# Expert tiles of two sizes in a decoder layer: 31 tiles of 256 rows and nine of 128, half tiles with the rows stationary, routing counts made earlier

## The chip, the core and the metric

One core of one Trainium2 chip runs the whole program. The metric is the device time of one execution in microseconds (us). The core has TensorE (PE), VectorE (DVE), ScalarE (ACT), GpSimd (POOL) and the sync engine (SP), which here only issues DMAs.

## What is computed

A decoder layer over 32 sequences of 128 tokens, 256 channels (4096 tokens): self attention, cross attention, then a block with self attention and a mixture of experts, each followed by a layer norm. The part that the change touches is the mixture:

```python
logits = h2 @ router_w                                   # 8 experts
topw, topi = jax.lax.top_k(jax.nn.softmax(logits), 2)
topw = jax.nn.softmax(topw)
shared = silu(h2 @ sh_gate) * (h2 @ sh_up) @ sh_down     # d_ff 512
gate, up = h2 @ e_gate[e], h2 @ e_up[e]
eout[e] = (silu(gate) * up) @ e_down[e]
X + shared + sum over the token's two experts of topw * eout[e]
```

Matrix products are kept near float32 by splitting both factors into a rounded part (`_hi`) and a rest (`_lo`) and adding three products: hi x hi, hi x lo, lo x hi.

## The kernel before

`phase_a` does the attention stages, and stores each token's normalized row (`h2`) and the residual sum. `phase_b` is the mixture. Its work is cut into 55 **units** of 256 rows (`UT`): 13 units of the shared expert (`BEFORE`), 39 **tiles** of the routed experts (`TILES` = 2 x 4096 / 256 + 8 - 1), 3 more shared units. A tile holds rows of one expert only; since the counts of an expert are known only at run time, 39 tiles are enough for any routing, and an expert's last tile can be partly empty.

While the first shared units run, DVE chooses the two experts of each token (`choose_first`, `choose_second`), weighs them (`weigh`), and takes each token's rank in its expert from two matmuls that PE issues after the first unit (`ranked`). `count_tiles` and `find_slots` turn the ranks into slot numbers (`slot_index`), `place` makes the table of each tile's expert. POOL then scatters the 8192 rows by indirect DMA into `slots_scratch` (64 DMAs, L1554), each batch of four behind a count of gate-and-up halves. SP loads a tile's rows (`load_slots`) and its expert's three weight matrices, 1.5 MB (`load_expert`), three sets of raw weights deep.

All engines walk the units in the same order, each in its own program:

- PE, unit n: `gate_up(n, 0)` (gate and up for the first 256 of the 512 hidden channels; weights stationary, 256 rows moving), `turn(n + 1)` (four transposes of the next rows), `gate_up(n, 1)`, `down_unit(n - 1)` (two row blocks of 128, `act` stationary, weights moving).
- ACT: `silu_half(n, 0)`, `token_hi(n + 1)`, `product_hi(n, 0)`, `split(n, 2)`, `split(n + 1, 0)`, `split(n + 1, 1)` (the rounded parts of the weights), `silu_half(n, 1)`, `product_hi(n, 1)`.
- DVE: `product(n, 0)` (silu times up, L1450), `read_down(n - 2)` (for a tile: scaled by the token's weight, L1473), `token_lo(n + 1)`, `split_lo(n, 2)`, `split_lo(n + 1, 0)`, `split_lo(n + 1, 1)` (L1434), `product(n, 1)`.
- POOL, in tiles: `routed_lo(n, 0)` (`act_lo`, L1569), `add_tile(i - 2)` (two indirect DMAs that add a tile's rows into `total_scratch`, L1580, each tile's behind the landing of all earlier ones), `routed_lo(n, 1)`.

After the tiles the sums are loaded back into `acc`, normalized pair by pair (DVE moments, POOL root, ACT scaling) and stored.

## Time and profile before

| | |
|---|---|
| median of 3 runs | 1155.63 us (1154.27 to 1155.94) |
| the profiled execution | 1154.84 us, its span 1153.0 us |
| PE busy | 1076.8 us, 93% of the span |
| DVE, ACT, POOL busy | 805.8 (70%), 620.1 (54%), 551.0 (48%) us |
| attention stages, then the mixture | up to 617.8 us, from there on |
| the 13 first shared units, the 39 tiles | 617.8 to 742.3 us, 742.3 to 1100.4 us |

The profile is of one execution; its rows give for each engine what ran when, and what an idle time before an instruction ended with (`<-`). A pair such as 128x256 is partitions by elements. "x12" are twelve instructions merged into one row. In the rows, tiles that live in freed places carry the name of the place: `kept_weights` can be the silu result or a tile's rows, `kept_late` the scaled rows of a tile, `h_rows`, `raw_gate` and `w_raw` raw expert weights, `turned` the transposed rows.

### The profile page before, as it was taken

What the parts mean: (1) busy time and instruction counts of PE and PEld (TensorE: products, weight loads), DVE (VectorE), ACT (ScalarE), POOL (GpSimd) and SP (SyncE); (2) the same over time, 40 slices, a digit from 0 to 9 for tenths busy, and PEclk for the clock granted to TensorE, in tenths of its full rate; (3) what the DMA queues carried; (4) which work ended last, traced back from release to release, by engine and by line L of the source; (5) the groups of instructions that cost most, each with busy time, mean ns of one, the idle gap of its engine ahead of it and who ended that gap; (6) DMA issues with size and microseconds to landing.
All of it is one profiled execution on the core that took longest, in us unless ns stands there. A gap on an engine that the chain in (4) does not pass through costs nothing. (4 is left out here: it accounts for less than half of the span.)

```text
span 1153.0 us, 32693 instructions
## 1 busy us (share of the span) xinstructions
PE 1076.8 (93%) x13012; PEld 1011.7 (88%) x13012; DVE 805.8 (70%) x1367; ACT 620.1 (54%) x1266; POOL 551.0 (48%) x542
## 2 busy tenths in 40 slices
PE   3789999999999999999966999999999999999992
PEld 2678889989898989898865999999999999999992
DVE  1668778777778777788645644577777777777746
ACT  1244555555555555566544333466666666666635
POOL 4243334344343344434201477346666666666754
PEclk8999999999999999999986999999999999999996
DMA  7585455454654444541215422368878887878548
GB/s 211 101 192 106 94 95 107 114 115 91 131 111 91 120 108 74 103 71 35 93 38 167 165 102 97 125 202 230 239 232 236 231 226 219 224 233 230 139 76 244
DMA packets 294679, 167.73 MB, mean 145 GB/s; under 512 B 220688, under 2 KB 266000, under 8 KB 293648
## 3 DMA queue, kind: packets, MB, share of 16 engines
q1 hardware_dynamic: 278064, 141.05, 45.5%
q0 software_dynamic: 14880, 22.09, 9.4%
q10 hardware_dynamic: 1584, 2.49, 0.6%
q8 instruction: 104, 1.70, 0.6%
q14 instruction: 47, 0.39, 0.1%
HBM read 121.74 MB, written 54.15 MB: 153 GB/s over the span
## 5 line engine op out<-in xcount | busy, mean ns | idle before, releaser
L1580 POOL DMA_INDIRECT total_scratch<-kept_late,slot_meta x78 | 135.4, 1736 | 110.6 <-DMA total_scratch<-kept_late,slot_meta 58.5
L1450 DVE TENSOR_TENSOR prod<-kept_weights,up 128x512 f32<-128x512 f32 x110 | 75.2, 683 | 144.2 <-ACT kept_weights L1290 144.2
L1569 POOL TENSOR_TENSOR act_lo<-prod,act_hi 128x512 fp32r<-128x512 f32 x78 | 120.3, 1686 | 36.5 <-ACT act_hi L1297 36.5
L1297 ACT ACTIVATE act_hi<-prod 128x512 fp32r<-128x512 f32 x110 | 69.5, 632 | 111.1 <-DVE prod L1450 109.7
L1290 ACT ACTIVATE kept_weights<-gate 128x512 f32<-128x512 f32 x110 | 64.8, 589 | 110.6 <-PE up L1221 110.6
L678 ACT ACTIVATE p3t<-psum 128x512 f32<-128x512 f32 x128 | 68.8, 596 | 89.2 <-PE psum L527 89.2
L929 POOL TENSOR_TENSOR ctx_lo<-ctx_t,ctx_hi 128x512 fp32r<-128x512 f32 x16 | 20.6, 1288 | 139.8 <-ACT ctx_hi L588 139.8
L849 DVE TENSOR_REDUCE max<-psum 128x16 f32<-128x2048 f32 x32 | 73.3, 2292 | 18.2 <-PE psum L513 18.2
L368 PE MATMUL psum<-kept_room,x_hi 128*128 128x512 f32 (+1 forms) x256 | 62.4, 367 | 18.3 <-POOL x_lo L925 18.3
L1274 ACT ACTIVATE we_hi<-w_raw 128x1024 fp32r<-128x1024 f32 x78 | 77.7, 1044 | 0.0
L1221 PE MATMUL gate<-tok_hi,we_hi 128*128 128x256 f32 x312 | 67.7, 298 | 1.2 <-DVE we_lo L1434 0.7
L368 PEld LDWEIGHTS psum<-kept_room,x_hi 128*128 128x128 f32 x256 | 42.3, 197 | 25.7 <-issue 21.4
L872 DVE RECIPROCAL rden<-psum 128x256 f32<-128x256 f32 x32 | 56.2, 1757 | 10.1 <-PE psum L540 10.1
L1554 POOL DMA_INDIRECT slots_scratch<-h_rows,slot_index x56 | 55.0, 982 | 16.7 <-issue 12.5
L1221 PE MATMUL up<-tok_lo,we_hi 128*128 128x256 f32 x312 | 62.8, 283 | 0.0
L1221 PE MATMUL up<-tok_hi,we_hi 128*128 128x256 f32 x312 | 62.6, 282 | 0.0
L1221 PE MATMUL gate<-tok_lo,we_hi 128*128 128x256 f32 x312 | 62.5, 282 | 0.0
L1434 DVE TENSOR_TENSOR we_lo_place<-w_raw,we_hi 128x1024 fp32r<-128x1024 f32 x39 | 53.7, 1403 | 1.2 <-ACT we_hi L1274 0.3
L1434 DVE TENSOR_TENSOR we_lo<-w_raw,we_hi 128x1024 fp32r<-128x1024 f32 x39 | 53.4, 1396 | 1.2 <-ACT we_hi L1274 0.3
L925 POOL TENSOR_TENSOR x_lo<-x_t,x_hi 128x512 fp32r<-128x512 f32 x16 | 20.5, 1278 | 66.3 <-ACT x_hi L584 66.2
L1221 PEld LDWEIGHTS gate<-tok_hi,we_hi 128*128 128x128 f32 x312 | 47.6, 190 | 4.8 <-issue 3.8
L1237 PE MATMUL down<-we_hi,act_hi 128*128 128x256 f32 x312 | 50.2, 283 | 0.0
(277 smaller groups left out, 3404.7 us busy)
## 6 DMA issues: line engine op xcount, KB each, us to landing
w_raw<-in_w_gate SPq DMA_DIRECT2D x26, 512.0 KB, 3.6
w_raw<-in_w_up SPq DMA_DIRECT2D x26, 512.0 KB, 4.5
w_raw<-in_w_down SPq DMA_DIRECT2D x26, 512.0 KB, 6.2
slots_scratch<-in_empty SPq DMA_DIRECT2D x39, 258.0 KB, 3.8
kept_weights<-slots_scratch SPq DMA_DIRECT2D x39, 258.0 KB, 6.0
raw_gate<-in_w_gate SPq DMA_DIRECT2D x13, 512.0 KB, 3.6
h_rows<-in_w_up SPq DMA_DIRECT2D x13, 512.0 KB, 4.5
h_rows<-in_w_down SPq DMA_DIRECT2D x13, 512.0 KB, 6.2
```

Of the source, the lines that this page charges most:

```text
L368: mm = pe.matmul(dst, x(dk), y(dk), start=(n == 1), stop=(n == 3 * DK))
L678: act.activation(p3t[:, a, 4 * j:4 * j + 4, :], bank[f"s3t_{a}"][:, 512 * j:512 * (j + 1)].rearrange("p (h n) -> p h n", h=4), ACT.Exp)\
L849: half_step(dve.tensor_reduce(max3[:, a, :], bank[f"s3_{a}"].rearrange("p (h n) -> p h n", h=H), AX.X, ALU.max, negate=True))
L872: half_step(dve.reciprocal(rden3[:, a, :], bank[f"pv3_{a}"][:, DK * S:2 * DK * S]))
L1221: mm = pe.matmul(bank[:, fi * UT:(fi + 1) * UT], wp[:, kind, dk * DFF + f * P:dk * DFF + (f + 1) * P], hp[:, n % 2, dk, :], start=(m == 1) ...
L1274: act.activation(w_hi[:, kind, :], raw_of(use)[kind], ACT.Copy).then_inc(w_hi_done, 1)
L1290: act.activation(silu[:, h, :], gate[h][:, :], ACT.Silu).then_inc(silu_done, 1)
L1297: act.activation(act_hi[:, n % 2, h * FH:(h + 1) * FH, :], prod[:, h, :].rearrange("p (f n) -> p f n", f=FH), ACT.Copy).then_inc(act_hi_do ...
L1434: dve.tensor_tensor(w_lo[:, kind, :], raw_of(use)[kind], w_hi[:, kind, :].bitcast(F32), ALU.subtract).then_inc(w_lo_done, 1)
L1450: dve.tensor_tensor(prod[:, h, :], silu[:, h, :], up[h][:, :], ALU.mult).then_inc(prod_done, 1)
L1569: pool.tensor_tensor(act_lo[:, n % 2, h * FH:(h + 1) * FH, :], prod[:, h, :].rearrange("p (f n) -> p f n", f=FH), act_hi[:, n % 2, h * FH: ...
L1580: pool.indirect_dma_start(out=scratch["total"], out_offset=bass.IndirectOffsetOnAxis(ap=slot_meta[:, i % METAS, j, 0:1].bitcast(I32), axis=0),
```

## The change

The routed experts get `FULL` = 31 tiles of 256 rows and `HALF` = 9 tiles of 128 rows, 40 tiles and 56 units. An expert's rest of up to 128 rows goes to a half tile, a larger rest to a full tile while there are full ones left, else to two half ones. `ORDER` runs four full tiles, then nine times three full ones and a half one.

In a half tile, `gate_up` keeps the 128 rows stationary and moves 256 columns of weights, so its result has rows on the partitions; the products are computed in that form, `turn_products` (new, PE) transposes them, four transposes into the bank `turned`, and `half_hi` (ACT) and `half_lo` (DVE, from PSUM) take the place of `product_hi`, `product_lo` and of POOL's `routed_lo`. `turn_products(n)` stands at the end of unit n on PE, behind `down_unit(n - 1)`. A half tile has one row block in `turn`, `down_unit`, `read_down` and `add_tile`.

The counting is longer (two kinds of tiles), and `count_tiles` moves from unit 1's first half to unit 0's second half, behind `weigh`. The list of steps also fills 36 pieces of empty slots in place of 39.

```diff
-TILES = 2 * B * S // UT + E - 1
+FULL = 2 * B * S // UT - 1
+HALF = E + 1
+TILES = FULL + HALF
-ROWS = TILES * UT
+ROWS = FULL * UT + HALF * P
+EMPTY = -(-ROWS // UT)
...
+        ORDER = [*range(FULL - 3 * HALF), *(x for h in range(HALF) for x in (*range(FULL - 3 * (HALF - h), FULL - 3 * (HALF - h) + 3), FULL + h))]
...
+        def product_read(k):
+            n = k // 2
+            return (act_turned, halves_upto(n)) if is_half(n) else low_products(k)
...
+                        if is_half(n - 2):
+                            pe.wait_ge(half_lo_done, halves_upto(n - 2))
-                        for j in range(2):
+                        for j in range(parts_of(n)):
...
+                        if is_half(n):
+                            for m, (wp, hp, dk) in enumerate(terms):
+                                at = dk * DFF + h * FH * P
+                                mm = pe.matmul(bank[:, 0:FH * P], hp[:, n % 2, dk, 0:P], wp[:, kind, at:at + FH * P],
+                                               start=(m == 0), stop=(m == 3 * DK - 1))
+                            continue
...
+                def turn_products(n):
+                    pe.wait_ge(prod_done, 2 * n + 2)
+                    for f in range(FT):
+                        mm = pe.transpose(turned[n % 2][:, f * P:(f + 1) * P], prod[:, f // FH, f % FH * P:(f % FH + 1) * P], ident[:, :])
+                    mm.then_inc(act_turned, 1)
...
+                    if is_half(n):
+                        turn_products(n)
...
+                def half_hi(n):
+                    act.wait_ge(act_turned, halves_upto(n))
+                    act.wait_ge(down_ready, n - 1)
+                    act.activation(act_hi[:, n % 2, :, 0:P], turned[n % 2][:, :].rearrange("p (f n) -> p f n", f=FT), ACT.Copy)\
+                       .then_inc(act_hi_done, 2)
...
-                    product_hi(n, 0)
+                    if not is_half(n):
+                        product_hi(n, 0)
...
-                    product_hi(n, 1)
+                    if is_half(n):
+                        half_hi(n)
+                    else:
+                        product_hi(n, 1)
...
+                    step_of_route(dve.scalar_tensor_tensor(out=f["rest"], in0=f["full"], scalar=-float(UT), in1=count,
+                                                           op0=ALU.mult, op1=ALU.add))
+                    step_of_route(dve.tensor_scalar(f["large"], f["rest"], float(P), None, ALU.is_gt))
...
+                    step_of_route(dve.tensor_tensor(further, slot[:, :, :], by_token("full_rows"), ALU.is_ge))
+                    step_of_route(dve.tensor_tensor(further, further, by_token("half_base"), ALU.mult))
+                    step_of_route(dve.tensor_tensor(slot[:, :, :], slot[:, :, :], by_token("full_base"), ALU.add))
+                    step_of_route(dve.tensor_tensor(slot[:, :, :], slot[:, :, :], further, ALU.add))
...
-                ROUTING = {(0, 0): (choose_second,), (0, 1): (weigh,), (1, 0): (count_tiles, find_slots), (1, 1): (place,)}
+                ROUTING = {(0, 0): (choose_second,), (0, 1): (weigh, count_tiles), (1, 0): (find_slots,), (1, 1): (place,)}
...
+                def half_lo(n):
+                    dve.wait_ge(act_hi_done, 2 * n + 2)
+                    dve.tensor_tensor(act_lo[:, n % 2, :, 0:P], turned[n % 2][:, :].rearrange("p (f n) -> p f n", f=FT),
+                                      act_hi[:, n % 2, :, 0:P].bitcast(F32), ALU.subtract).then_inc(half_lo_done, 1)
...
                     product(n, 1)
                     if i is None:
                         product_lo(n, 1)
+                    elif is_half(n):
+                        half_lo(n)
...
-                    routed_lo(n, 0)
+                    if not is_half(n):
+                        routed_lo(n, 0)
                     if i >= 2:
                         add_tile(i - 2)
-                    routed_lo(n, 1)
+                    if not is_half(n):
+                        routed_lo(n, 1)
```

## Rows read from the trace of the kernel before

**Rows 1.** Busy time by stretch: PE, PEld, DVE, ACT, POOL; clock, DMA share, GB/s.
```profile
617.00:644.00 27.00, 23.20 (x155) 22.82 (x156) 20.97 (x48) 11.16 (x17) 1.63 (x2) 0.82 0.41 132
...
860.00:940.00 80.00, 79.98 (x663) 78.85 (x663) 59.64 (x80) 50.80 (x79) 53.09 (x36) 1.00 0.82 234
```

**Rows 2.** Chain that ended last, first tile: start us, us, what.
```profile
742.50 1.44 PE gate L1221 x12
...
745.82 1.43 PE gate L1221 x12
...
748.69 2.88 PE down L1237 x24
751.57 1.42 PE gate L1221 x12
```

**Rows 3.** PE in order of time: start us, us, instruction, count, [idle before, releaser].
```profile
736.09 0.66 PE L1201 MATMUL turned<-ident,kept_weights 128*128 128x128 f32 x4 [1.02 <-DMA slot_meta<-slots_scratch]
...
742.34 0.40 PE L1221 MATMUL gate<-tok_hi,we_hi 128*128 128x256 f32 x2
...
1100.43 0.40 PE L1221 MATMUL gate<-tok_hi,ws_hi 128*128 128x256 f32 x2
```

**Rows 4.** DVE in order of time, the first tile and one in the middle.
```profile
746.05 0.69 DVE L1450 TENSOR_TENSOR prod<-kept_weights,up 128x512 f32<-128x512 f32 x1 [2.58 <-ACT kept_weights L1290]
...
748.39 1.48 DVE L1434 TENSOR_TENSOR we_lo<-w_raw,we_hi 128x1024 fp32r<-128x1024 f32 x1 [0.26 <-ACT we_hi L1274]
749.79 2.35 DVE L1434 TENSOR_TENSOR we_lo_place<-w_raw,we_hi 128x1024 fp32r<-128x1024 f32 x2
752.06 0.68 DVE L1450 TENSOR_TENSOR prod<-kept_weights,up 128x512 f32<-128x512 f32 x1
...
882.34 0.69 DVE L1450 TENSOR_TENSOR prod<-kept_weights,up 128x512 f32<-128x512 f32 x1 [2.16 <-ACT kept_weights L1290]
...
884.68 1.86 DVE L1434 TENSOR_TENSOR we_lo_place<-w_raw,we_hi 128x1024 fp32r<-128x1024 f32 x1
...
888.73 0.68 DVE L1450 TENSOR_TENSOR prod<-kept_weights,up 128x512 f32<-128x512 f32 x1
```

**Rows 5.** ACT in order of time, around the start of a tile.
```profile
880.21 0.63 ACT L1297 ACTIVATE act_hi<-prod 128x512 fp32r<-128x512 f32 x1 [2.21 <-DVE prod L1450]
881.71 0.60 ACT L1290 ACTIVATE kept_weights<-gate 128x512 f32<-128x512 f32 x1 [0.87 <-PE up L1221]
```

**Rows 6.** POOL in order of time, the same tile and the next.
```profile
879.06 1.95 POOL L1580 DMA_INDIRECT total_scratch<-kept_late,slot_meta  x1 [2.84 <-DMA total_scratch<-kept_late,slot_meta]
881.31 1.55 POOL L1580 DMA_INDIRECT total_scratch<-kept_late,slot_meta  x1 [0.30 <-issue]
882.32 3.12 POOL L1569 TENSOR_TENSOR act_lo<-prod,act_hi 128x512 fp32r<-128x512 f32 x2
888.12 2.13 POOL L1580 DMA_INDIRECT total_scratch<-kept_late,slot_meta  x1 [2.68 <-issue]
```

**Rows 7.** DVE and POOL in order of time, the routing.
```profile
638.03 0.68 DVE L1389 TENSOR_TENSOR_SCAN w_raw<-w_raw,down 128x256 f32<-128x256 f32 x1
...
640.30 0.17 DVE L1400 TENSOR_TENSOR_SCAN tiles_upto<-w_raw,n_tiles 128x8 f32<-128x8 f32 x1
640.51 0.17 DVE L1404 TENSOR_TENSOR first_row<-tiles_upto,n_tiles 128x8 f32<-128x8 f32 x1
...
644.02 0.19 POOL L1549 COPY kept_rows<-row_w 128x4 f32<-128x4 f32 x1 [25.17 <-DVE slot_index L1412]
```

**Rows 8.** POOL, then DVE, in order of time behind the tiles.
```profile
1113.39 1.55 POOL L1580 DMA_INDIRECT total_scratch<-kept_late,slot_meta  x1 [0.30 <-issue]
1117.37 3.65 POOL L1598 DMA_DIRECT2D acc<-total_scratch  x4 [2.43 <-DMA total_scratch<-kept_late,slot_meta]
...
1131.12 0.69 DVE L1467 TENSOR_TENSOR acc<-down,acc 128x512 f32<-128x512 f32 x1 [0.85 <-PE down L1237]
...
1139.30 0.75 DVE L1482 BATCH_NORM_STATS2 stats_b<-acc 128x6 f32<-128x256 f32 x2 [1.02 <-DMA acc<-total_scratch]
```

More of the change, by code:

```diff
@@ L1036, in phase_b @@
         past = late[:, E * SHARED:E * SHARED + TILES * E].rearrange("p (i e) -> p i e", e=E)
+        few = {n: sb(n, [P, E]) for n in ("full", "full_upto", "rest", "large", "large_upto", "grown", "half", "half_upto", "over",
+                                          "full_base", "half_base", "full_rows")}
         expert_iota = c["expert"].rearrange("p (b e) -> p b e", e=E)
@@ L1231, in down_unit @@
                         pe.wait_ge(down_read, n - 1)
-                    for j in range(2):
+                    for j in range(parts_of(n)):
                         m = 0
@@ new lines, in count_tiles @@
+                    step_of_route(dve.scalar_tensor_tensor(out=f["half"], in0=f["rest"], scalar=0.0, in1=f["large"],
+                                                           op0=ALU.is_gt, op1=ALU.add))
+                    step_of_route(dve.scalar_tensor_tensor(out=f["half"], in0=f["grown"], scalar=-2.0, in1=f["half"],
+                                                           op0=ALU.mult, op1=ALU.add))
+                    step_of_route(dve.tensor_tensor(f["full"], f["full"], f["grown"], ALU.add))
```

115 lines of the change are left out of this document (73 added, 42 removed).

## The prediction

> **What bounds the kernel now.** I read three views in order. First the busy time by stretch [rows 1]: in the middle of the expert tiles PE is busy for the whole stretch at the full clock, DVE three quarters of it, and the DMA engines 0.82. So the stage is PE's, if nothing holds PE back unseen. Second, the chain of work and PE's own order of time [rows 2, 3]. A unit of 256 rows is a first gate-and-up half with the turning of the next rows (742.50 to 745.82, 3.32), a second one (2.87) and the products down of the unit before (2.88): 9.07 us. The 39 tiles take 1100.43 - 742.34 = 358.1 us, 9.18 each. Third, DVE's order of time [rows 4], because a PE that is always busy may have another engine running exactly as fast. The product `prod` of the first half starts 3.71 after the unit (742.34 to 746.05), that of the second half 6.01 later (to 752.06), or 6.39 later (882.34 to 888.73). Between them DVE scales the rows of the tile two before, makes `tok_lo` and splits three weight matrices, 1.14 each when alone (2.35 for two). The next unit may start when the second of these three is done: 3.71 + 6.01 - 1.14 + 0.1 for the signal = 8.7, or 9.05 in the longer form. This loop through PE, ACT and DVE is only 0.0 to 0.4 us shorter than PE's own work. That is what the reader is to see: a stage with 100% of PE busy and a second bound right beneath it, which does not shrink with the rows of a tile, since it is made of weight splits.
>
> Why two forms: the subtraction of POOL (L1569) and the first split of DVE overlap. In the short form that split takes 1.48, in the long form 1.86, where POOL ran two subtractions in one piece until 885.4 [rows 4, 6]. The Trainium skill, page "SBUF — State Buffer", section "Who interferes with whom", says that a DVE instruction with two SBUF inputs blocks, and is blocked by, a GpSimd instruction that reads SBUF; by that rule the trace agrees, and `half_lo`, which reads PSUM and SBUF, would not collide.
>
> **The tiles.** The 39 units become 31 full ones and nine half ones: four full, then nine times three full and one half. I call the half one H, the full ones behind it F1, F2 and F3.
>
> PE alone: a half tile has 12 + 12 matmuls of gate and up instead of 48, 12 down instead of 24, and 4 + 2 transposes instead of 4. By [rows 2] that is 1.44 + 1.44 + 1.44 + 0.44 + 0.22 = 4.98 against 9.07. If PE alone counted, the stage would be 31 x 9.05 + 9 x 4.98 = 325.4, some 33 us less. I don't take it, for this reason.
>
> H: its PE sequence is gate-and-up 1.44, turning 0.44, gate-and-up 1.44, then the *full* products down of F3 (2.88), then the new `turn_products`, which waits for both products. In front of the second product stand, in DVE's program, all three splits. The working: `prod` of F3's second half starts 3.71 + 6.01 to 6.39 - 0.28 (its `tok_lo` is for a half tile) = 9.44 to 9.82 after F3's start, that is 0.6 to 1.0 into H. Then come this product (0.68), `act_hi` (0.63, partly overlapped) and the silu of H, 0.35 as half of the 0.60 [rows 5]: 1.6 in sum. From the first to the second product of H: 6.01 - 0.27 for the half product - 0.27 as POOL has no subtraction of H, 5.5; at worst 6.1. Product 0.43, four transposes 0.44. Sum: 8.6 to 9.6 us, against PE's own 6.6. I take 8.8, near the lower end, because only the one subtraction for F3 is left in H and it starts at H + 3 at the latest by [rows 6] if an add holds it less than now. PE's queue behind the waiting transpose is the first gate of F1; who waits for it is everybody.
>
> F1 has the short products down (1.44 less), so PE needs 7.6; but its splits are whole: 8.7 by the loop. F2: PE 9.05 with an occasional delay, 9.1; its scaling of H's rows is 0.4 shorter, which nobody feels. F3: 9.05 less two transposes 0.22 = 8.83, the loop 8.8; I take 8.85. Group: 8.8 + 8.7 + 9.1 + 8.85 = 35.45, bounds 34.9 and 36.3. The stage: 4 x 9.05 = 36.2, plus 9 x 35.45 = 319.05, plus 0.35 (the first F1 has no H before it), less 1.0 (the last H has no splits of a next tile in front of its product) = **354.6, against 358.1: -3.5 us**. So nearly all of the 33 us is spent on 40 tiles' splits instead of 39, each at the pace of the loop.
>
> What hides the rest: the forty weight loads. A group has four loads in 35.4 us, now four in 36.7, and 3.5 instead of 4 tiles of slots and adds; the share of 0.82 [rows 1] stays where it is, and loads are issued two and a half units ahead. SP's `load_slots` behind H's early `load_expert` may wait up to 3 us for an add; the rows are needed over 10 us later. The adds of POOL: each must land before the next, 881.31 to 888.12, 6.8 us, and with two issues a tile makes 879.06 to 888.12, 9.06 [rows 6]; this chain is as long as a unit too. H's tile has one issue, 2.25 less, so per group it is 4 x 9.06 - 2.25 = 34.0, within 35.45. If that cover goes, see the second rival.
>
> **The start.** `count_tiles` began at 638.03 and is now done behind `weigh`, 632.3. It has ten small steps more, and `find_slots` nine small ones in place of two, of 0.21 each (640.30 to 640.51), and three more over 256 columns, 0.45 each [rows 7]. From 632.3: the old part 2.3 and 2.1 of new steps, 636.7; then the product, `tok_lo` and `act_lo` that stood in front before (2.1), 638.8; then 1.9 + 1.8 + 2.5 = 6.2, 645.0. The slot numbers, for which POOL waits until 644.02, were there at 643.9: **+1.1 us** (bounds 0 and +2.5, as a step on an [128, 8] tile with a column operand is in no row). All of it counts: POOL's 64 scatters follow without a pause, and PE waits for the first rows (1.02, [rows 3]).
>
> **The tail.** The last tile is a half one; its products down stand in the first shared unit behind the tiles: PE is 1.44 earlier, and the `acc` of DVE at 1131.12 with it. The last adds: one issue less at their end, and about 4 us earlier against PE's unit, so the wait of 1.02 for the sums [rows 8] goes; DVE and ACT are next. **-2.4 us** (bounds 0 and -2.5). The 36 instead of 39 fills of empty slots lie in the first stage beside PE's work: nothing.
>
> **Sum.** -3.5 + 1.1 - 2.4 = -4.8. The profiled execution is 1154.84 (span 1153.0, 1.84 around it), 0.8 under the median 1155.63: span 1148.2, that execution 1150.0, median **1150.8**.
>
> **Rivals.**
> 1. The long form everywhere, and H at 9.45 (slower). POOL's subtraction for F3 starts only when its add is issued, 881.31 + 1 = unit + 3.7, and then meets the first split of H as it does now [rows 4, 6]. Group 36.3: +7.7, 1158.5. For it: the long form holds through most of the tiles. Against: the chain of adds gets 1.4 us of air per group. It decides from a group of 35.98 on, where the sum is zero.
> 2. One add per load burst. If an add lands when the burst of weights ends, as two of 6.8 suggest beside lone ones at the tail (1113.39 to 1117.1, [rows 8]), a unit can't be under 9.2: 40 x 9.2 - 1.4 = 366.6, 12 more, 1162.8.
> 3. PE's clock. The granted clock is 0.82 in a stretch where PE idles 3.8 of 27 us [rows 1]. H leaves PE idle for some 2 us in two pieces. If each H put the next twelve matmuls to the lower level, 1.2 GHz, they would take 2.88 instead of 1.44 [rows 2], 9 x 1.44 = 13 more at most: 1163. Against: the 1.02 us of wait at 736.09 was followed by gates of 1.44 at 742.50, the full clock [rows 2, 3]. The Trainium skill, page "TensorE: Matmul & The Clock Gate", Part 1, says that the slow clock is the default and that activity releases it; no run here shows yet which of the two an H is.
> 4. PE's own work sets the pace after all: 325.4, 1121. It needs DVE to be some 3.3 us earlier in H and 1.1 in F1, and no row shows such room.
> 5. The short form throughout, H 8.5: group 35.0, 1146.7.
>
> **How the numbers follow.** Forecast with its own bounds (1146 to 1154) 0.46; rival 1, partly reached in many mixtures (1154 to 1160), 0.27; rival 2, 0.08; rival 3, 0.03; rival 4, 0.04; rival 5, 0.12. A measurement of this kernel tells about 0.2% (2.3 us) from no change, 1153.3 to 1157.9. Faster: nine tenths of the forecast, rivals 4 and 5, 0.58; same: the forecast's last tenth and over half of rival 1, 0.20; slower: the rest of rival 1, rivals 2 and 3, 0.22. The range takes rival 1 and the better end of the others: 1144 to 1162; its own for the forecast is 1146 to 1154.
>
> **What would show it.** In the changed kernel PE must be idle before `turned<-prod` for about a microsecond in each H, released by DVE's `prod`; an H must take 8.6 to 9.1, F1 8.7; DVE's first split 1.2 to 1.5 in H and F1. The scatter must begin at about 646; the chain must have no 1.02 wait for `acc`. Wrong would be: H near 6.6, F1 near 7.6 (rival 4), a granted clock under 1 in the tiles (rival 3), or a wait of PE for `act_lo` in front of the products down (rival 2).

## The result, and the profile after

The change makes the kernel slower: 1162.26 us median over 15 runs beside 1155.94 for the kernel before, ratio 1.0056 with the interval [1.0041, 1.0071]; the forecast was 1150.8, its range 1144 to 1162. One run of each kernel took far longer (2603.03 and 2117.05 us) and is in the medians but not in the ratio; the others lie from 1157.85 to 1166.54 and from 1154.18 to 1157.59. The profiled execution took 1158.89, its span 1157.0. It is one of the shorter ones, so the profile shows less of the loss than the median.

| span of the profile, us | before | after | difference | forecast |
|---|---|---|---|---|
| up to the first tile | 742.34 | 743.62 | +1.3 | +1.1 |
| the tiles | 358.1 | 362.9 | +4.8 | -3.5 |
| behind the tiles | 52.6 | 50.5 | -2.1 | -2.4 |

The execution takes 1.9 us more than its span, as before (1.84). Start and tail came nearly as forecast; the error is in the tiles. Read from the starts of the units (the first `gate` of each in PE's order of time), the 40 tiles take, in us (H in bold; ahead of the first group stand four full ones of 9.06, 9.01, 9.04, 8.98):

| F1 | F2 | F3 | H |
|---|---|---|---|
| 9.03 | 9.24 | 8.87 | **10.71** |
| 8.90 | 9.23 | 8.88 | **10.48** |
| 8.88 | 9.07 | 8.82 | **8.75** |
| 8.88 | 9.08 | 8.81 | **8.75** |
| 8.89 | 9.08 | 8.81 | **8.78** |
| 8.95 | 9.07 | 8.82 | **8.75** |
| 8.88 | 9.08 | 8.81 | **9.74** |
| 8.88 | 9.08 | 8.81 | **10.48** |
| 10.24 | 9.24 | 8.90 | **7.14** |

So the undisturbed group is 8.88 + 9.08 + 8.81 + 8.75 = 35.5, against 35.45 forecast. Four H, the late ones from here on, are longer by 1.96, 1.73, 0.99 and 1.73, and one F1 by 1.36: 7.8 us, which is nearly the whole distance between 354.6 and 362.9. (The last H has no next tile to split weights for, and is short as forecast.)

**The H that went as forecast, and the one that did not.** PE in order of time in the changed kernel (start us, us, instruction, count, [idle before, releaser]), first the late H that starts at 806.85:

```profile
808.72 0.60 PE L1235 MATMUL turned<-ident,kept_weights 128*128 128x128 f32 x4
...
812.77 0.71 PE L1281 MATMUL down<-we_hi,act_hi 128*128 128x256 f32 x4 [2.03 <-issue]
...
813.83 1.06 PE L1281 MATMUL down<-we_hi,act_lo 128*128 128x256 f32 x4
...
817.21 0.60 PE L1267 MATMUL turned<-ident,prod 128*128 128x128 f32 x4
```

and the same places in the H that starts at 881.82:

```profile
886.38 0.71 PE L1281 MATMUL down<-we_hi,act_hi 128*128 128x256 f32 x4 [0.67 <-issue]
890.16 0.66 PE L1267 MATMUL turned<-ident,prod 128*128 128x128 f32 x4 [0.67 <-DVE prod L1549]
```

The second one has the wait that I looked for, 0.67 us for DVE's `prod` ahead of the new transposes, and the length that I gave it. But even here PE also waits 0.67 before the products down; in the late one that is 2.03. What it waits for stands in POOL's order of time, the same two tiles:

```profile
807.95 1.56 POOL L1685 DMA_INDIRECT total_scratch<-kept_late,slot_meta  x1 [3.46 <-DMA slot_meta<-slots_scratch]
809.81 1.56 POOL L1685 DMA_INDIRECT total_scratch<-kept_late,slot_meta  x1 [0.30 <-issue]
810.81 1.86 POOL L1675 TENSOR_TENSOR act_lo<-prod,act_hi 128x512 fp32r<-128x512 f32 x1
...
880.85 2.25 POOL L1685 DMA_INDIRECT total_scratch<-kept_late,slot_meta  x1 [1.39 <-DMA slot_meta<-slots_scratch]
883.41 1.56 POOL L1685 DMA_INDIRECT total_scratch<-kept_late,slot_meta  x1 [0.30 <-issue]
884.42 1.86 POOL L1675 TENSOR_TENSOR act_lo<-prod,act_hi 128x512 fp32r<-128x512 f32 x1
```

The second `act_lo` of F3 stands behind F1's add (the add of the tile two before), and that behind the landing of the adds before it. It starts 2.6 us into the normal H and 3.96 into the late one, and ends at 812.67 there; PE starts down at 812.77. In a full unit the products down stand 6.2 behind its start and there is room for this; in H they stand behind only 3.9 us of work. (`issue` as releaser hides it: PE's program waits there for `act_lo`.)

**What the late `act_lo` costs at the full clock.** Not this wait. In the H of 9.74, which starts at 1024.01 and waits 1.80 at down, PE is done with down and then still waits for DVE's second product:

```profile
1033.34 0.66 PE L1267 MATMUL turned<-ident,prod 128*128 128x128 f32 x4 [0.55 <-DVE prod L1549]
```

POOL's `act_lo` and DVE's first split in this H, then the same split in the normal one:

```profile
1027.73 1.86 POOL L1675 TENSOR_TENSOR act_lo<-prod,act_hi 128x512 fp32r<-128x512 f32 x1
1028.47 2.21 DVE L1532 TENSOR_TENSOR we_lo_place<-w_raw,we_hi 128x1024 fp32r<-128x1024 f32 x1
...
886.28 1.22 DVE L1532 TENSOR_TENSOR we_lo_place<-w_raw,we_hi 128x1024 fp32r<-128x1024 f32 x1
```

The split is begun beside the subtraction and ends 1.09 behind its end (1029.59), as if it had run after it. It takes 1.0 us more than in the normal H (2.21 beside 1.22), the product behind it starts 1.0 later (8.87 behind the start of H, 7.86 in the normal one), and H is 1.0 longer. The four late H have this split at 2.44, 2.21, 2.21 and 2.21, no other H has it over 1.22. This is the meeting of rival 1, in four groups of nine.

**The clock.** Busy time by stretch: PE, PEld, DVE, ACT, POOL; clock, DMA share, GB/s; the products down of the H of 10.71 in two pieces, those of the normal one, and those of the H of 9.74:

```profile
812.80:815.20 2.40, 2.40 (x15) 2.40 (x16) 2.40 (x3) 0.51 (x2) 0.00 (x0) 0.69 0.67 106
815.20:817.20 2.00, 2.00 (x11) 2.00 (x11) 1.16 (x2) 0.00 (x0) 1.55 (x1) 0.52 0.69 227
886.40:890.10 3.70, 3.09 (x24) 2.88 (x24) 3.70 (x4) 1.87 (x3) 0.00 (x0) 1.00 1.14 275
1029.70:1033.30 3.60, 3.09 (x24) 2.89 (x24) 3.59 (x4) 0.76 (x2) 0.00 (x0) 1.00 0.94 189
```

In the H of 10.71 the granted clock falls to about the half (1.2 GHz) about a microsecond after PE is back from its wait, and the 24 matmuls take 4.44 us, where they take 2.84 in a full unit (804.01 to 806.85). Here the wait at down does count: the slow products end behind `prod`, and `turned<-prod` has no wait (817.21). The clock fell in three of the four late H (waits of 2.03, 1.79 and 1.79), and not in the fourth (1.80): 10.48 beside 9.74.

**The F1 of 10.24.** POOL adds the tile F2 of the last group but one; the second issue of that add falls into F1 of the last group, and the `act_lo` behind it onto a split of DVE:

```profile
1069.47 1.56 POOL L1685 DMA_INDIRECT total_scratch<-kept_late,slot_meta  x1 [3.37 <-DMA total_scratch<-kept_late,slot_meta]
1077.16 1.55 POOL L1685 DMA_INDIRECT total_scratch<-kept_late,slot_meta  x1 [6.13 <-issue]
1078.17 1.84 POOL L1675 TENSOR_TENSOR act_lo<-prod,act_hi 128x512 fp32r<-128x512 f32 x1
1078.34 2.76 DVE L1532 TENSOR_TENSOR we_lo_place<-w_raw,we_hi 128x1024 fp32r<-128x1024 f32 x1
```

and PE's first row of the next tile, F2:

```profile
1081.24 0.47 PE L1259 MATMUL gate<-tok_hi,we_hi 128*128 128x256 f32 x2 [2.39 <-DVE we_lo_place L1532]
```

Between the two issues of one tile's add there is 0.30 us of idle time everywhere else (809.81, 883.41). Here it is 6.13, and the profile names no reason. I call it the held DMA; it was in none of my steps, and the later experiments are about it.

**What stayed.** The rest answers to rows of the kernel before. The stretches of [rows 1]:

```profile
617.00:644.00 27.00, 22.39 (x156) 21.87 (x157) 24.54 (x64) 11.84 (x18) 1.79 (x2) 0.83 0.43 138
860.00:940.00 80.00, 73.99 (x607) 72.27 (x606) 57.85 (x82) 50.71 (x81) 47.27 (x30) 1.00 0.77 223
```

PE's wait for the first rows, as in [rows 3]:

```profile
737.37 0.66 PE L1235 MATMUL turned<-ident,kept_weights 128*128 128x128 f32 x4 [1.27 <-DMA slot_meta<-slots_scratch]
```

DVE's last step of the slot numbers and POOL's first one behind it, as in [rows 7] (two rows, one of each engine's order of time):

```profile
644.76 0.18 DVE L1508 CAST slot_index<-row_slot 128x32 int32<-128x32 f32 x1
...
645.06 0.19 POOL L1655 COPY kept_rows<-row_w 128x4 f32<-128x4 f32 x1 [25.46 <-DVE slot_index L1508]
```

POOL's last add and first load of the sums, as in [rows 8]:

```profile
1117.80 1.55 POOL L1685 DMA_INDIRECT total_scratch<-kept_late,slot_meta  x1 [3.07 <-DMA total_scratch<-kept_late,slot_meta]
1122.40 3.67 POOL L1705 DMA_DIRECT2D acc<-total_scratch  x4 [3.05 <-DMA total_scratch<-kept_late,slot_meta]
```

and DVE's first sum of the last units, and its wait for the sums:

```profile
1135.84 0.69 DVE L1571 TENSOR_TENSOR acc<-down,acc 128x512 f32<-128x512 f32 x1 [0.85 <-PE down L1281]
1143.53 0.75 DVE L1586 BATCH_NORM_STATS2 stats_b<-acc 128x6 f32<-128x256 f32 x2 [0.53 <-DMA acc<-total_scratch]
```

In 860 to 940, which holds no late H, PE is busy 74.0 of 80 us where it was 80.0: the work that the half tiles save is there as idle time, and the stage does not run faster for it.

### The profile page after: what moved, and what is told of

Its sections match the earlier page's. It is cut to its first block and busy times, and to the rows that moved or that the text cites. A ratio compares the mean times of both kernels' runs of the same rounds, so it can differ in the third digit from the quotient of the medians.

```text
span 1157.0 us, 32256 instructions
## 1 busy us (share of the span) xinstructions
PE 1059.0 (92%) x12782; PEld 990.8 (86%) x12782; DVE 804.7 (70%) x1396; ACT 614.4 (53%) x1266; POOL 521.6 (45%) x519
## 5 line engine op out<-in xcount | busy, mean ns | idle before, releaser
L1549 DVE TENSOR_TENSOR prod<-kept_weights,up 128x512 f32<-128x512 f32 (+1 forms) x112 | 71.7, 640 | 129.1 <-ACT kept_weights L1337 129.0
L1675 POOL TENSOR_TENSOR act_lo<-prod,act_hi 128x512 fp32r<-128x512 f32 x62 | 93.5, 1534 | 60.6 <-ACT act_hi L1344 60.5
L1337 ACT ACTIVATE kept_weights<-gate 128x512 f32<-128x512 f32 (+1 forms) x112 | 62.2, 556 | 109.5 <-PE up L1259 109.5
L1344 ACT ACTIVATE act_hi<-prod 128x512 fp32r<-128x512 f32 x94 | 59.4, 632 | 91.5 <-DVE prod L1549 90.7
L373 PE MATMUL psum<-kept_room,x_hi 128*128 128x512 f32 (+1 forms) x256 | 63.3, 371 | 18.1 <-POOL x_lo L930 18.1
L1259 PE MATMUL gate<-tok_hi,we_hi 128*128 128x256 f32 x248 | 53.7, 298 | 9.8 <-DVE we_lo_place L1532 9.8
L1281 PEld LDWEIGHTS down<-we_hi,act_hi 128*128 128x128 f32 x284 | 40.4, 198 | 11.7 <-issue 11.6
L941 POOL TENSOR_TENSOR x_res<-x_res,b_o 128x512 f32<-128x512 f32 x16 | 21.1, 1318 | 65.1 <-DMA x_res<-in_x 65.1
L1259 PE MATMUL up<-tok_lo,we_hi 128*128 128x256 f32 x248 | 49.9, 283 | 0.0
L1259 PE MATMUL up<-tok_hi,we_hi 128*128 128x256 f32 x248 | 49.8, 282 | 0.0
L1259 PE MATMUL gate<-tok_lo,we_hi 128*128 128x256 f32 x248 | 49.7, 282 | 0.0
```

What stands on the lines that cost most here:

```text
L373: mm = pe.matmul(dst, x(dk), y(dk), start=(n == 1), stop=(n == 3 * DK))
L1259: mm = pe.matmul(bank[:, fi * UT:(fi + 1) * UT], wp[:, kind, dk * DFF + f * P:dk * DFF + (f + 1) * P], hp[:, n % 2, dk, :], start=(m == 0) ...
L1281: mm = pe.matmul(down[n % 2][:, j * D:(j + 1) * D], ap[:, n % 2, f, j * P:(j + 1) * P], wp[:, 2, f * D:(f + 1) * D], start=(m == 1), stop= ...
L1337: act.activation(used(silu[:, h, :], n), used(gate[h][:, :], n), ACT.Silu).then_inc(silu_done, 1)
L1549: dve.tensor_tensor(used(prod[:, h, :], n), used(silu[:, h, :], n), used(up[h][:, :], n), ALU.mult).then_inc(prod_done, 1)
L1675: pool.tensor_tensor(act_lo[:, n % 2, h * FH:(h + 1) * FH, :], prod[:, h, :].rearrange("p (f n) -> p f n", f=FH), act_hi[:, n % 2, h * FH: ...
```

## The experiments

The ratios are to the kernel before, run on the same chip. The diffs are to the changed kernel unless the text names another one, and show only the lines that make the difference. The length of units is that of the profiled execution.

**The order of POOL.** In F3, its second `act_lo` is issued ahead of the add.

```diff
+                    if is_half(n + 1):
+                        routed_lo(n, 1)
                     if i >= 2:
                         add_tile(i - 2)
-                    if not is_half(n):
+                    if not is_half(n) and not is_half(n + 1):
                         routed_lo(n, 1)
```

> The changed kernel, but in the unit before each half tile POOL makes its second act_lo ahead of the adds. Theory A (in four of nine half tiles PE waited about 2 us at the products down because the act_lo of F3 stood in POOL's program behind adds that were still landing, and the clock then fell): all H at 8.7 to 8.9, full clock in the tiles, 1150 to 1153 us, small spread. Theory B (the pace is only the second product behind the splits): H that were slow stay slow, time as the changed kernel, 1158 to 1166. Theory A with the chain of adds as the next bound: H are mended, but PE waits for act_lo in F2 instead, 1154 to 1160.

Measured: 1232.36, ratio 1.0656 [1.0631, 1.0681]. Every H but the last is 8.72 to 8.75: the wait at down and the long split are gone, so it was this `act_lo`. But from the second group on every F2 takes 18.1 to 20.0 us. POOL in order of time:

```profile
857.19 1.56 POOL L1685 DMA_INDIRECT total_scratch<-kept_late,slot_meta  x1
859.05 2.60 POOL L1685 DMA_INDIRECT total_scratch<-kept_late,slot_meta  x1 [0.30 <-issue]
869.20 1.75 POOL L1685 DMA_INDIRECT total_scratch<-kept_late,slot_meta  x1 [7.55 <-DMA total_scratch<-kept_late,slot_meta]
...
882.07 3.07 POOL L1675 TENSOR_TENSOR act_lo<-prod,act_hi 128x512 fp32r<-128x512 f32 x2
```

PE in the F2 that starts at 870.79:

```profile
884.01 1.19 PE L1281 MATMUL down<-we_hi,act_hi 128*128 128x256 f32 x4 [6.85 <-issue]
```

The add starts 3.8 us behind the start of H (853.41), where in the changed kernel it starts between 1.0 ahead of it and 1.1 behind; its second issue lands after 9.4 us, and the next adds and `act_lo` all stand behind that. The chain of adds has little air: what is given away ahead of it comes back as 9 to 11 us in each F2. A part of this is the clock, at half behind such waits (the first four matmuls of down take 1.19 where they take 0.71 in the H above).

**H's second product ahead of the next tile's splits** (on ACT its silu, on DVE its product).

```diff
+                    if is_half(n):
+                        product(n, 1)
                     if tile_next:
                         split_lo(n + 1, 0)
                         split_lo(n + 1, 1)
-                    product(n, 1)
+                    if not is_half(n):
+                        product(n, 1)
```

> The changed kernel, but in a half tile ACT makes the second silu and DVE the second product before the splits of the next tile. Theory B: H falls from 8.75 by about 1.1 to 7.6, after which the splits for F1 end last; nine times 1.1 makes 10 us less. Theory A: this gain comes only where the act_lo of F3 is early; where PE waits for it at 5.9 us into H, the products down end at 8.8 and H gains at most 0.3 to 1, so 3 to 6 us less than the changed kernel, 1154 to 1160, and the clock still falls.

Measured: 1162.11, 1.0062 [1.0039, 1.0085], the same as the changed kernel. Three of the first eight H are 7.85 to 7.87, where POOL is in time, the others 9.0 to 11.0, and the F2 of the last group is 13.16. In the late H the wait at down now costs at the full clock too (9.0 instead of 7.87), as nothing of DVE ends behind it. So the loop through DVE is what gave the normal H its 8.75, as forecast, and taking it away alone is worth nothing while the wait at down and the held DMA remain.

**The move of the counting alone**, on the kernel before:

```diff
-                ROUTING = {(0, 0): (choose_second,), (0, 1): (weigh,), (1, 0): (count_tiles, find_slots), (1, 1): (place,)}
+                ROUTING = {(0, 0): (choose_second,), (0, 1): (weigh, count_tiles), (1, 0): (find_slots,), (1, 1): (place,)}
```

> The kernel before, and only count_tiles moved behind weigh. The moved steps take 2.7 us and fit ahead of the first product of unit 1 with no delay; find_slots ends at 641.2 instead of 643.9. If the scatter sets the start of the tiles: 2.5 to 2.8 us less, ratio 0.9977. If PE's own units 0 to 12 set it: only the 1.0 us that PE waited for the rows, ratio 0.9991.

Measured: 1153.76, 0.9975 [0.9960, 0.9990]. The scatters begin at 640.92 instead of 644.02 [rows 7], the first tile at 741.11 instead of 742.34: 3.1 us at the source and 1.2 at PE, where the wait of 1.02 for the first rows [rows 3] is now 0.46. The ratio says 2.9 us (1.2 to 4.6), as the first expectation had it; the first tile moved as the second one had it, and 0.7 more lies in the tiles of this execution (357.4 us beside 358.1). Where the rest comes from isn't shown. The reverse edit, the changed kernel with the counting back in unit 1:

> The changed kernel with count_tiles back in unit 1 behind act_lo. The move is worth what its steps take in front of find_slots: 4.4 us, of which 0.7 had delayed the first product. Slot numbers at 648.6 instead of 644.9, the first tile and the end 3.7 us later, 1166; if PE's units hide part of it, 1163 to 1165.

Measured: 1168.83, 1.0105 [1.0079, 1.0131]. The scatters begin at 650.41, the first tile at 748.96: 5.3 us later than in the changed kernel, where 3.7 was expected. The longer routing thus costs 6.4 us (650.41 - 644.02) and the move gives 5.3 back; my +1.1 was the difference of the two. In this run the F2 of the last group took 15.49.

**Work for PE in the wait.** Twelve matmuls whose result nobody reads, ahead of the wait before H's products down.

```diff
+                    if n + 1 < UNITS and is_half(n + 1):
+                        for m in range(12):
+                            pe.matmul(turned[(n + 1) % 2][:, 0:D], act_hi[:, n % 2, m % 2, 0:P], w_hi[:, 2, m % 2 * D:(m % 2 + 1) * D],
+                                      start=True, stop=True)
```

> The changed kernel with twelve matmuls (1.4 us) whose result is not used, in each half tile between gate-and-up and the wait in front of the products down. If the granted clock falls because PE stands idle there: the clock is full in all tiles, H that waits costs 9.7 instead of 10.5 to 10.7, 2 to 4 us less than the changed kernel. If the fall has to do with the half tile's other idle time or not with idling: clock under 1 in some H as before, time unchanged. H without a wait stays at 8.75, as the products down still end before DVE's second product.

Measured: 1161.28, 1.0055 [1.0034, 1.0076]. The late H are now 10.10, 9.77, 9.77, 9.77, the others 8.74 to 8.75 but for the last. One stretch with two late H, in this kernel:

```profile
779.00:860.00 81.00, 77.63 (x636) 75.84 (x635) 59.38 (x81) 48.97 (x77) 49.05 (x31) 1.00 0.79 230
```

and in the changed one:

```profile
779.00:860.00 81.00, 75.93 (x602) 74.61 (x601) 58.01 (x79) 47.17 (x76) 47.77 (x30) 0.96 0.79 230
```

With PE kept at work the clock doesn't fall in any H, and a late one costs 1.0 us (once 1.35) instead of 1.7 (once 1.96). What stays is the long split: it takes 2.23 (once 2.57), and in each late H PE waits 0.56 for `prod` behind down. The fall costs 0.6 to 0.7 for each of three late H, 2 us in all. (In the last group, behind a wait of 2.18 without such matmuls, the clock fell here too.) By what the Trainium skill says in "TensorE: Matmul & The Clock Gate", Part 1, the slow clock is the default and activity releases it; the two lines above agree.

**The same `act_lo` on another engine.** In F3, DVE makes the second `act_lo`, POOL's order is kept.

```diff
+                def edge_lo(n):
+                    dve.wait_ge(act_hi_done, 2 * n + 2)
+                    dve.tensor_tensor(act_lo[:, n % 2, FH:FT, :], prod[:, 1, :].rearrange("p (f n) -> p f n", f=FH),
+                                      act_hi[:, n % 2, FH:FT, :].bitcast(F32), ALU.subtract).then_inc(edge_lo_done, 1)
...
+                    elif is_edge(n):
+                        edge_lo(n)
```

> The changed kernel, but the second act_lo of each full tile ahead of a half one is made by DVE (in its 0.97 us of idle time ahead of the half tile's first product), not by POOL; the adds keep their order. Theory A (act_lo behind the adds holds PE in H): no H over 9.2, each H 8.75 to 9.1 as the first product of H comes 0.35 later, clock 1.00 but at the ends of the tiles, 4 to 6 us less than the changed kernel (1156 to 1158). Theory that the adds' chain bounds the pace wherever the wait shows: H mended and F1 or F2 longer by the same, time as the changed kernel, 1162.

Measured: 1168.66, 1.0119 [1.0084, 1.0154]. No H waits at down, all but the last are 9.06 to 9.09: the 0.69 of subtraction on DVE makes H's own product later. One F1 is 10.38: there the clock fell behind a wait of 1.90 for `prod`, which it did not behind seven such waits of 1.90 to 1.92 in the other H. The F2 of the last group is 17.52, with 6.77 us of wait for `act_lo`. With both edits, this one and H's product first:

> The same as x8_edge_lo and in H also the second product ahead of the next tile's splits, as in x2_product_first. If both holds are gone and nothing else ends last: H 7.9 to 8.2, nine times 0.9 us less than x8, 1148 to 1151, below the kernel before (1156). If the adds bound the pace: four units of a group need 4 x 9.06 - 2.25 = 34.0 at least; H + F1 + F2 + F3 = 8.0 + 8.9 + 9.1 + 8.85 = 34.9 lies just over it, so some groups show a wait for act_lo in F2 and half the gain stays out, 1152 to 1156.

Measured: 1157.38, 1.0018 [1.0005, 1.0031]. Every H but the last is 7.61 to 7.63, 1.13 us less than the normal H of the changed kernel, 9 us over the nine and half of the way to PE's own 6.6. It isn't faster than the kernel before all the same: F1 and F2 rise to between 8.9 and 10.6 in many groups. PE waits there for DVE's splits, five of which take 2.2 to 2.8, begun beside an `act_lo` of POOL that a late add had pushed back; behind two of these waits (1.77 and 2.25) the clock fell. And F2 of the last group is 17.98. POOL there:

```profile
1066.95 1.55 POOL L1705 DMA_INDIRECT total_scratch<-kept_late,slot_meta  x1 [5.42 <-DMA total_scratch<-kept_late,slot_meta]
1073.97 1.82 POOL L1705 DMA_INDIRECT total_scratch<-kept_late,slot_meta  x1 [5.47 <-issue]
1075.24 1.86 POOL L1695 TENSOR_TENSOR act_lo<-prod,act_hi 128x512 fp32r<-128x512 f32 x1
```

and PE:

```profile
1086.59 1.20 PE L1288 MATMUL down<-we_hi,act_hi 128*128 128x256 f32 x4 [6.85 <-issue]
```

**Less to load.** From the fourth tile on only a sixteenth of each `w_down` matrix is loaded; the kernel computes with what is in the place, so its result is no longer the layer's. First in the changed kernel, then in the one with both edits.

```diff
-                        sp.dma_start(raws[i % 3][k], t[n][bass.ds(e, 1), :, :].rearrange("a p n -> (a p) n"))\
+                        cols = slice(0, 64) if k == 2 and i >= 3 else slice(0, WC)
+                        sp.dma_start(raws[i % 3][k][:, cols], t[n][bass.ds(e, 1), :, cols].rearrange("a p n -> (a p) n"))\
```

> The changed kernel, but from the fourth tile on only 64 of the 1024 columns of each w_down matrix are loaded (the rest stays from an earlier tile), a third of the weight traffic less. If the adds land late because they share the DMA engines with the weight loads: landing 4.5 to 5.5 us instead of 6.6 to 8.4, no H over 8.9, no fall of the clock, the long form of the other units gone (F2 9.03), span 1148 to 1151. If landing has its own length: landing as before, slow H as before, span 1157 or more.

Measured, in a single run: 1156.54. All H but the last are 8.72 to 8.75, with the clock up. The span is 1154.6, not under 1151, as the F2 of the last group takes 14.04.

> This is x9_edge_product, and from the fourth tile on only 64 of the 1024 columns of each w_down matrix are loaded (the kernel leaves that part of the loading out, and computes with what is in the place; all instructions of the engines stay). Theory 1, the landing of an add is stretched by the loads of weights, and the adds, each behind the landing of all earlier ones, are what makes F1 and F2 9.2 to 10.6 us: landings 6.0 to 6.4, F1 at 8.65, F2 at 9.1, 8 to 12 us less than x9, 1145 to 1149, the held issue of the last group still there (F2 13 to 15). Theory 2, the order of issues sets these units whatever is loaded: within 2 us of x9, 1155 to 1159.

Measured: 1148.42, 0.9931 [0.9912, 0.9950]. DMA issues from 779 to 1095 (operation, queue, count, median us from issue to landing), in the kernel with both edits:

```profile
total_scratch<-kept_late,slot_meta POOLq DMA_INDIRECT x62, 6.6
```

and with less to load:

```profile
total_scratch<-kept_late,slot_meta POOLq DMA_INDIRECT x65, 6.2
```

F1 is 8.6 to 9.0 in all groups and F2 9.0 to 9.2 in the first eight, and no split takes over 2 us. So what made them 9.2 to 10.6 was the load of weights. That it acts through the landing of the adds is argued: 0.4 us in the median is little, but each tile's add stands behind the one before, so over the four of a group it is 1.6 us (an estimate), and an add that lands late makes the next late. Only the F2 of the last group remains, 16.52. It doesn't hang on these loads.

**Which add is held.** I then counted. From the first scatter on, the late second issue is the 125th indirect DMA of POOL in each kernel so far, and the 125th is late in the kernel before too, where it is the first issue of an add. POOL there, and in it the unit that starts at 1044.86 takes 9.85:

```profile
1046.36 1.55 POOL L1580 DMA_INDIRECT total_scratch<-kept_late,slot_meta  x1 [3.87 <-issue]
...
1050.95 2.48 DVE L1434 TENSOR_TENSOR we_lo_place<-w_raw,we_hi 128x1024 fp32r<-128x1024 f32 x1
```

What it waits for is seen from the landing of the 124th, asked for alone in each trace. In the changed kernel the 124th (1069.47) lands after 7.2 us, and the 125th starts 0.5 behind that. So it is in all ten traces in which the 125th is the second issue of an add: it starts 0.4 to 0.5 us behind the landing of the first, while every other second issue of every trace follows its first with 0.30 or 0.31 of idle time. In the kernel before most of the 3.87 is a wait that every first issue has, as the program lets it wait for all adds before: the others start 0.7 to 0.8 behind the last landing, the 125th 1.5. With the 0.7 more POOL's two subtractions reached further into a split of DVE, which took 2.48 (1050.95).

Three full tiles ahead of the groups and one behind, in the kernel with both edits:

```diff
-        ORDER = [*range(FULL - 3 * HALF), *(x for h in range(HALF) for x in (*range(FULL - 3 * (HALF - h), FULL - 3 * (HALF - h) + 3), FULL + h))]
+        ORDER = [0, 1, 2, *(x for h in range(HALF) for x in (3 * h + 3, 3 * h + 4, 3 * h + 5, FULL + h)), FULL - 1]
```

> This is x9_edge_product with three full tiles ahead of the nine groups and one behind them, in place of four and none. Counted from the first scatter, the 125th indirect DMA of POOL was issued late in every kernel so far, the one before the change among them (3.87 us of idle time that nothing explains there, 5.3 to 6.1 in those with half tiles); in those it was the second issue of F2's add in the last group, with act_lo of F1 behind it. With this order the 125th is the first issue of F3's add, which stands 5 to 7 us for a landing anyway. Theory 1, the hold belongs to the count and hides behind the landing: no unit over 11 us in the last group, where x9 had one of 17.98; 8 to 9 us less than x9, 1149 to 1151 (the last tile is a full one again, +1.4). Theory 2, it belongs to the place near the end or to the last group: a unit of 15 to 18 us stays, 1157 to 1160.

Measured: 1157.01, 1.0011 [0.9997, 1.0025]. I had miscounted: ahead of the eighth group of nine stand 6 + 7 x 7 = 55 issues, so the 61st, the 125th DMA, is the *second* issue of its F3, which POOL makes in F1 of the ninth. It is the one held, no longer F2's, which puts the count above the place in the group:

```profile
1061.56 2.00 POOL L1705 DMA_INDIRECT total_scratch<-kept_late,slot_meta  x1 [1.66 <-DMA total_scratch<-kept_late,slot_meta]
1070.46 1.72 POOL L1705 DMA_INDIRECT total_scratch<-kept_late,slot_meta  x1 [6.89 <-issue]
```

and the unit that it falls into takes 15.73. Between the two issues lie 8.9 us here, 7.7 in the changed kernel, 7.0 with both edits, and the first of the two landed after 8.4, 7.2 and 6.6. With two full tiles ahead and two behind, the 125th is the first issue of an add, which waits for the landing of all earlier ones anyway:

```diff
+        ORDER = [0, 1, *(x for h in range(HALF) for x in (3 * h + 2, 3 * h + 3, 3 * h + 4, FULL + h)), FULL - 2, FULL - 1]
```

> This is x9_edge_product with two full tiles ahead of the nine groups and two behind. In x13_shift_order the 125th indirect DMA was again the one held, and it was again the second issue of a tile (6 + 7 x 7 = 55 issues ahead of the last group; the 61st add is F3's second), 8.9 us behind the first one, which is as long as a landing. Here 4 + 2 x 3 ... the 61st add is the first issue of F1 in the last group (4 + 8 x 7 = 60 ahead of it), which waits for the landing of all earlier adds anyway. Theory 1, the 125th waits until what was issued before it has landed: nothing is lost, no unit over 11 us in the last two groups, 8 to 9 us less than x9 and 7 less than x13, 1148 to 1151. Theory 2, it is held by some 6 us in any place: POOL idle for 10 us or more ahead of that add, a unit of 13 us or more, 1155 to 1158.

Measured: 1172.99 beside 1180.17 for the kernel before on this chip, 0.9935 [0.9919, 0.9951]. The longest unit of the stage is 9.63, the 40 tiles take 768.33 to 1118.16 = 349.8 us. POOL in the last group:

```profile
1083.82 2.27 POOL L1705 DMA_INDIRECT total_scratch<-kept_late,slot_meta  x1 [2.53 <-DMA total_scratch<-kept_late,slot_meta]
...
1093.08 1.89 POOL L1705 DMA_INDIRECT total_scratch<-kept_late,slot_meta  x1 [2.90 <-issue]
```

The 125th (1093.08) comes 9.3 us behind the one before and 1.6 behind its landing, and delays nobody. Of the versions that compute the layer this is the fastest here.

**The order alone**, without the two edits, in the changed kernel:

> This is the changed kernel with two full tiles ahead of the nine groups and two behind, in place of four and none; nothing else differs. It tells how much of the loss is the 125th indirect DMA of POOL (held until what was issued before it has landed) and how much is the wait of PE for act_lo in H with the fall of the clock behind it. Theory 1, each has a share: the slow H units of 9.7 to 10.7 us stay in half of the groups (4 to 8 us in sum), the units behind the 61st add are normal: 2 to 5 us less than the changed kernel, 1.0015 to 1.0040 of the kernel before. Theory 2, the held DMA is nearly all of it: at or under the kernel before, 0.9960 to 1.0000. Theory 3, it is the waits in H alone: no difference to the changed kernel, 1.0050 or more.

Measured: 1182.33 beside 1179.77, 1.0019 [1.0005, 1.0033]. Three H are late (10.48, 9.75, 10.48), no other unit is over 9.1, the tiles take 360.5. Against 1.0056 the order is worth 0.37%, 4.3 us, with some 0.2% of doubt by the two intervals; I take it for the held DMA, though the order may also have spared one late H (three instead of four in the profiled executions). From 1.0019 to 0.9935 the two edits give 0.84%, 9.7 us.

**The matmuls of down that need no `act_lo`, first**, on the kernel before with the earlier counting:

```diff
-                    pe.wait_ge(*low_products(2 * n + 1))
+                    pe.wait_ge(act_hi_done, 2 * n + 2)
...
+                            if j == 0 and ap is act_lo:
+                                pe.wait_ge(*low_products(2 * n + 1))
```

> This is the kernel before with two edits: count_tiles behind weigh, as in x4_before_ranks, and the products down take the four hi x hi and four lo x hi matmuls of the first row block before they wait for act_lo. Theory 1, PE does not wait for act_lo in the kernel before except in one or two units, so the second edit is worth 0 to 1 us: 1152.8 to 1153.8, the same as x4 within its interval. Theory 2, PE's starts of the products down are the loop's second bound in many units: 2 to 4 us less than x4, 1150 to 1152.

Measured: 1156.39, 1.0004 [0.9992, 1.0017]: no gain, and 0.3% above the move of the counting alone, which I did not expect. PE never waits at down in the tiles of the kernel before or of this one with the earlier counting alone, so the edit had nothing to take. Three units are long (9.89, 10.18, 10.09), and in the first the cause is a split of DVE that is begun beside POOL's two subtractions (974.80 to 977.90), in place of 1.2 to 1.5 us:

```profile
976.47 2.52 DVE L1436 TENSOR_TENSOR we_lo_place<-w_raw,we_hi 128x1024 fp32r<-128x1024 f32 x1
```

Whether the edit brings such meetings about or they fell so in this execution is open; the kernel before has three units over 9.4 as well.

## Why the prediction was wrong, point by point

- **The start, +1.1: right.** +1.04 at POOL and +1.28 at the first tile. Of the new steps, small ones took 0.20 each and those over 256 columns 0.46, as taken from [rows 7].
- **The tail, -2.4: right**, -2.1. DVE's wait for the sums did not go, though, it is 0.53 instead of 1.02: the last add is issued 11.3 us behind the last tile instead of 13.0, 1.7 earlier where I took 4. What the tail gave is these 0.5 and PE's shorter last products, by which the first `acc` is 1.4 earlier against the end of the tiles.
- **PE alone is not the pace (rival 4): right.** H has PE idle 1.3 us and more, and the loop through PE, ACT and DVE gives 8.75, where I took 8.8. That this loop holds H is shown by H at 7.62 once its product stands ahead of the splits. F1 8.88 (8.7 taken), F2 9.08 (9.1), F3 8.81 (8.85). F1 has the short form, as taken (its first split is 1.48, at 896.69). What it takes more is the product's start at 3.79 instead of 3.71, the second split's end (1.21 behind its start, where I counted 1.14) and 0.15 from there to PE instead of 0.1.
- **The step that failed** is the choice of 8.8 for H, near the lower end, because POOL's one subtraction "starts at H + 3 at the latest by [rows 6] if an add holds it less than now". In four of the first eight H it started at 2.6. In the other four an add held it to 3.7 to 3.96, and it met DVE's first split of H: 2.21 to 2.44 us instead of 1.22, H's product 1.0 to 1.2 later, H at 9.7 to 10.0 without any fall of the clock. That is the mechanism of rival 1, in H though not in F1 or F2, and it is 4.2 us.
- **A step that was missing:** I did not set `act_lo` against the new place of the products down. In H they stand 3.9 us behind the start where a full unit has 6.2, and `act_lo` stands behind an add that may be issued at +1.1: 1.10 + 1.86 + 1.00 + 1.86 = 5.82. That gives a wait of 0.67 in a normal H and of 1.8 to 2.0 in the four late ones. At the full clock both are hidden by the later `prod`; what the long ones cost is the clock. Rival 2 had named this very sign, a wait for `act_lo` ahead of down, but with an add per load burst as the pace; the adds' chain was late only at times, not in each unit.
- **The clock (rival 3)** had the mechanism and a chance of 0.03, with 13 us as its most (1150.8 + 13 is 1163.8, not 1163). It is 0.7 for each of three H, 2.2 us, and it comes from the wait at down, of which that rival knew nothing. The waits of 0.67 in the normal H, at down and for `prod`, were never followed by a fall.
- **The adds' cover, 34.0 within 35.45: the term was right on average and wrong as a cover.** A group's adds fit, but each add that lands late shifts the next, and POOL's `act_lo` waits in that chain. With less to load no H was late.
- **The held DMA was in no step.** A trace of it was to be seen before, 3.87 us of idle time with no named reason and a unit of 9.85, though all but 0.7 of it is the wait that each first issue has; I had read such units as "an occasional delay". The new tiles turned it from a first issue, where it hides behind a landing, into a second one with an `act_lo` behind it. By the kernel with the other order it is up to 4.3 us of the loss at the median.
- In sum: four long splits 4.2, the clock 2.2, the F1 behind the held DMA 1.4 make the 7.8 us of the profiled execution. The median is 3.4 above it, and the other kernels whose last F2 takes 13 to 18 us show where such executions may lose it. That this is what the longer executions of the changed kernel itself have is argued from those; none of them was profiled.

## What to carry to other kernels

When a stage gets a unit of another size, don't only add up its work: list for each engine how far behind the unit's start each step stands, and set every producer on another queue against it, the slow in-order one (here POOL with its adds) first. Ask of a late producer also what it then runs beside: here the wait that it caused was hidden, and the split of DVE that it slowed was not. A queue whose steps wait for DMA landings has no spare time that an average can show, and an odd number of issues can turn a stall that was hidden into one that isn't. Then the order in which the units run counts as well as the work that they save: two full tiles moved from the front to the end gave some 0.4%, with the same work.

## What the runs showed of the hardware

- The 125th indirect DMA that POOL issues is held until the one before has landed. In the ten traces in which it is a second issue it starts 0.4 to 0.5 us behind that landing, after 4.5 to 6.9 us of idle time, where every other second issue follows after 0.30 or 0.31. In the five in which it is a first issue (2.9 to 3.9 us of idle time, 1.5 to 1.6 behind the landing, where others have 0.7 to 0.8) it costs little. The 91st, 100th and 114th show `issue` as well in some traces (888.12 in [rows 6]; 945.25 and 1016.57 in the changed kernel), but only where they are first or single issues, 1.0 to 1.4 behind a landing; as second issues they have 0.30. The count was varied through the order of the tiles alone, not by further DMAs, so that it is the count and not something that grows with it is well supported and not proved. Nothing in the profile names the resource.
- A DVE split that is begun beside POOL's subtraction ends 1.1 us behind the end of the subtraction: so do all 48 splits of these traces that took over 2 us beside one, 45 begun while it ran and three up to 0.5 us ahead of it (2.06 to 4.68 us instead of 1.22; 1028.47 and 1050.95 above).
- A wait of PE inside dense work can be followed by half the clock. Over the tiles of all 15 traces, by the granted clock of the 4 us behind the wait: behind 24 waits of 1.37 to 1.75 us the clock never fell, behind 34 of 1.77 to 2.39 it fell 16 times, behind 13 of 3.77 and more each time. Waits of 1.79 and 1.80 in the same place of the same kernel were followed by either (1066.20 and 1029.69), so the length of the wait alone does not decide. Twelve unused matmuls in the wait prevented the fall in four late H.
- Indirect adds of 128 rows land 6.2 to 7.2 us behind their issue in the median, in stretches in which the DMA engines move 168 to 232 GB/s in all; behind the tiles, in the kernel before, the last ones take 3.6 to 3.8. The longest of all traces took 9.9, in the kernel with POOL's order changed.
